# Load stage with split constants and two issuing queues, and the first expert's gathers moved into the routing block

## The reference, cut to what matters

```python
    logits = jnp.einsum('bsh,eh->bse', x, router_w) + router_b
    topk_vals, topk_idx = jax.lax.top_k(softmax(logits), 2)
    ...
    sorted_indices = jnp.argsort(-expert_mask, axis=0)[:cap]        # cap = 512
    used_idx = (sorted_indices * sorted_mask).reshape(-1)
    inputs = x_flat[used_idx] * sorted_mask                          # rows gathered by index
    h = relu(einsum('ceh,ehi->cei', inputs, experts_inter))          # 7 experts, 128 -> 512
    out = einsum('cei,eih->ceh', h, experts_out) * in_w              # 512 -> 128
    combined = zeros.at[used_idx].add(out)                           # rows scattered by index
    combined = combined + x_flat * (noop_w * noop_mask)
    ...
    x = x + layernorm(attention(layernorm(x), Wq, bq, Wk, bk, Wv, bv, Wo, bo))   # the first layer
```

## Time and profile before

| | us |
|---|---|
| median of three runs | 1279.82 |
| lowest and highest of them | 1271.53, 1280.86 |
| the profiled execution, its own time | 1281.18 |
| its span in the trace | 1279.4 |
| the load block, to the first instruction of the next | 15.16 |
| `route`, to the first instruction of `capped_mixture` | 1124.01 to 1157.29 |
| `capped_mixture`, to the end | 1157.29 to 1279.4 |

### The profile page before, as it was taken

The page is one execution under the profiler, slowest core; times in us unless marked ns, Lnnn a source line. Parts: engine busy times, 40 slices in busy tenths (PEclk is TensorE's granted clock), DMA queues, the critical chain, the costliest instruction groups (busy, mean ns, idle before and its releaser), DMA issues. The chain is left out here.

```text
span 1279.4 us, 33612 instructions
## 1 busy us (share of the span) xinstructions
PE 1126.1 (88%) x11807; PEld 633.0 (49%) x11807; DVE 997.9 (78%) x2742; ACT 849.6 (66%) x1826; POOL 657.2 (51%) x680
## 2 busy tenths in 40 slices
PE   3879999999999997999999999789999999617766
PEld 2334444444444443566666666445666665414552
DVE  2679999999999983888898889459999998782213
ACT  1468888888888885555555565268999998522204
POOL 3213444454433310556655666547888887505653
PEclk9889999999999998999999999899999999858987
DMA  4231111111111110000000000013122111041117
GB/s 113 62 93 32 32 28 30 32 31 28 34 32 31 34 30 1 2 2 2 2 1 2 1 2 1 4 37 96 49 56 55 37 40 31 18 133 34 44 40 197
DMA packets 83141, 48.91 MB, mean 38 GB/s; under 512 B 17111, under 2 KB 80032, under 8 KB 82976
## 3 DMA queue, kind: packets, MB, share of 16 engines
q1 hardware_dynamic: 80496, 42.62, 12.5%
q0 software_dynamic: 1792, 3.70, 1.1%
q10 hardware_dynamic: 688, 0.44, 0.1%
HBM read 16.51 MB, written 10.26 MB: 21 GB/s over the span
## 5 line engine op out<-in xcount | busy, mean ns | idle before, releaser
L577 DVE TENSOR_REDUCE mxsS<-scoreS 128x2 f32<-128x512 f32 x512 | 329.0, 685 | 44.0 <-PE scoreS L685 38.8
L473 ACT ACTIVATE PTS<-stS 128x512 f32<-128x512 f32 x512 | 283.4, 591 | 58.4 <-PE stS L689 58.2
L1833 POOL TENSOR_TENSOR ghid<-gprod,ghid 128x512 f16<-128x512 f32 x144 | 165.4, 1159 | 122.3 <-ACT ghid L1946 120.7
L685 PE MATMUL scoreS<-QK 31*128 31x256 f16 x1024 | 170.9, 282 | 27.6 <-DVE mxsS L577 12.0
L885 POOL TENSOR_TENSOR PTP<-PTP,EP 128x512 f32<-128x512 f32 x128 | 162.8, 1283 | 53.0 <-ACT PTP L1061 52.8
L689 PE MATMUL stS<-QK 32*128 32x256 f16 x1024 | 167.2, 279 | 1.3 <-ACT PTS L473 1.3
L705 PE MATMUL pvS<-PTS,Vx 128*32 128x256 f32 x2048 | 141.1, 394 | 0.6 <-ACT PTS L473 0.4
L1946 ACT ACTIVATE ghid<-gprod 128x512 f16<-128x512 f32 x144 | 90.1, 626 | 69.8 <-DVE gprod L2041 69.7
L1215 DVE TENSOR_SCALAR AP<-score_psP 128x768 int32<-128x768 int32 x128 | 121.6, 950 | 17.3 <-PE score_psP L1354 16.5
L685 PEld LDWEIGHTS scoreS<-QK 31*128 31x128 f16 x1024 | 53.1, 93 | 148.1 <-DVE mxsS L577 90.2
L1061 ACT ACTIVATE PTP<-AP,epsP 128x768 f32<-128x768 f32 x128 | 119.2, 931 | 3.0 <-DVE AP L1215 2.4
(11 more groups left out here) (322 smaller groups left out, 2244.0 us busy)
## 6 DMA issues: line engine op xcount, KB each, us to landing
QK<-HLS SPq DMA_DIRECT2D x384, 32.0 KB, 1.9
QK<-HLP SPq DMA_DIRECT2D x192, 32.0 KB, 1.9
expert_outputs<-tzero SPq DMA_DIRECT2D x8, 512.0 KB
cgot<-expert_outputs SPq DMA_DIRECT2D x16, 256.0 KB, 5.2
tokens<-XB SPq DMA_DIRECT2D x16, 128.0 KB, 2.8
out_dram<-X SPq DMA_DIRECT2D x8, 256.0 KB, 2.3
wi<-L_ffn_experts_inter_dram SPq DMA_DIRECT2D x1, 1792.0 KB, 8.4
wo<-n_L_ffn_experts_out_dram SPq DMA_DIRECT2D x7, 256.0 KB, 3.3
```

Source lines behind the costliest of these rows:

```text
L473: act.activation(PT[:, n % NPT, :], st_ps[:, (NS * t + n) % 3, :], ACT.Exp, scale=SCALE).then_inc(s_exp, 1)
L577: dve.tensor_reduce(mxs[:, u // 4, :, at], score_ps[:, n % 2, :].rearrange("p (c s) -> p c s", c=TC), AX.X, ALU.max).then_inc(s_max, 1)
L685: scored = pe.matmul(score_ps[:, k, cols], QK[part, new, g, 0, rows], QK[part, new, g, 1, :], start=True, stop=True)
L1833: pool.tensor_tensor(hid[:, n // FC % NHID, 1, c, :], prod[:, n % NPROD, :], hid[:, n // FC % NHID, 0, c, :], ALU.subtract).then_inc(s_hid, 1)
```

## The change

In the load block the constants come as two DMAs, the identity first. A new semaphore `s_first` counts that piece and the four weights of the first layer; PE waits for these five (80) and turns four weights. DVE then waits for the rest (`s_rows` at 64: three weights, second piece of constants, two gates) ahead of `spread_v`; PE's matmuls with `wo` and the biases and DVE's copies of `bo` and `bias1` come next, and the other three weights and the gates are turned and copied last. The seven late loads leave SP's list and stand at the end of ACT's, behind the copies of `ones`.

In `route`, POOL waits for `s_clear` (9 DMAs) and for DVE's index casts and issues the four gathers of expert 0 there, on a semaphore `s_xe0` that is allocated outside both blocks. `capped_mixture` begins with gather 1. PE gets 16 matmuls without a reader at the end of `route` and keeps 4 of its 24 in `capped_mixture`.

```diff
@@ load_weights
         def _(sp):
             for k, src in enumerate([dram["L0_attn_Wq"], dram["L0_attn_Wk"], dram["L0_attn_Wv"], dram["L0_attn_Wo"]]):
-                sp.dma_start(rows[:, k, :], src).then_inc(s_rows, 16)
+                sp.dma_start(rows[:, k, :], src).then_inc(s_first, 16)
...
-            for k, name in enumerate(["L0_ffn_wq", "L0_ffn_wk", "L0_ffn_wv"]):
-                sp.dma_start(arriving.flat[:, k, :], dram[name]).then_inc(arriving.s_flat, 16)
-            sp.dma_start(weights[1]["wo"][:], dram["L0_ffn_wo"]).then_inc(arriving.s_flat, 16)
-            sp.dma_start(arriving.route0[:], dram["L0_ffn_router_w"]).then_inc(arriving.s_flat, 16)
-            sp.dma_start(w["norm2"][:], dram["L0_ffn_norm2_w"].rearrange("(d a) -> d a", a=1)).then_inc(arriving.s_flat, 16)
-            sp.dma_start(arriving.norm[:, 0:1], dram["L0_ffn_norm1_w"].rearrange("(d a) -> d a", a=1))\
-                .then_inc(arriving.s_flat, 16)
 
         @block.scalar
         def _(act):
-            act.dma_start(cst[:], dram["constants"]).then_inc(s_rows, 16)
+            act.dma_start(cst[:, 0:C_TRI], dram["constants"][:, 0:C_TRI]).then_inc(s_first, 16)
+            act.dma_start(cst[:, C_TRI:C_ALL], dram["constants"][:, C_TRI:C_ALL]).then_inc(s_rows, 16)
...
             for k in range(3):
                 act.dma_start(QK[SHIFT_LAST:P:32, k, :, 1, :], ones[:]).then_inc(s_one, 16)
+            for k, name in enumerate(["L0_ffn_wq", "L0_ffn_wk", "L0_ffn_wv"]):
+                act.dma_start(arriving.flat[:, k, :], dram[name]).then_inc(arriving.s_flat, 16)
...
             act.wait_ge(s_one, 48)
...
         def _(pe):
-            pe.wait_ge(s_rows, 128)
-            for k in range(len(names)):
+            pe.wait_ge(s_first, 80)
+            for k in range(4):
                 pe.transpose(turned[:, k, 0:P], rows[:, k, :], cst[:, 0:P]).then_inc(s_turned, 1)
-            pe.transpose(turned[:, 7, 0:H + NE], gates[:], cst[0:H + NE, 0:H + NE]).then_inc(s_turned, 1)
-
             pe.wait_ge(s_spread, 1)
...
+            pe.wait_ge(s_rows, 64)
+            for k in range(4, len(names)):
+                pe.transpose(turned[:, k, 0:P], rows[:, k, :], cst[:, 0:P]).then_inc(s_turned, 1)
+            pe.transpose(turned[:, 7, 0:H + NE], gates[:], cst[0:H + NE, 0:H + NE]).then_inc(s_turned, 1)
...
             dve.wait_ge(s_bias, 80)
+            dve.wait_ge(s_rows, 64)
             dve.tensor_scalar(spread_v[:], cst[:, C_TRI + P:C_TRI + 2 * P], bias_v[:, 0:1], None, ALU.mult)\
                .then_inc(s_spread, 1)
+            dve.wait_ge(s_out, 1)
+            dve.tensor_copy(weights[0]["bo"][:], turned[:, 0, 0:D])
+            dve.wait_ge(s_out, 2)
+            dve.tensor_copy(w["bias1"][:], turned[:, 1, 0:NE])
             for k, name in ((4, "wq"), (5, "wk")):
...
-            dve.wait_ge(s_out, 1)
-            dve.tensor_copy(weights[0]["bo"][:], turned[:, 0, 0:D])
-            dve.wait_ge(s_out, 2)
-            dve.tensor_copy(w["bias1"][:], turned[:, 1, 0:NE])
@@ route
             pool.wait_ge(s_zero, 5)
+            pool.wait_ge(s_clear, 16 * (2 * NT * D // (P * 1024) + 1))
+            pool.wait_ge(s_v, marks["index"])
+            for t in range(CAP // P):
+                pool.indirect_dma_start(xe[:, 0, t, :], None, yd, bass.IndirectOffsetOnAxis(ap=idx_in[:, t:t + 1], axis=0),
+                                        bounds_check=NT - 1, oob_is_err=False).then_inc(s_xe0, 16)
...
             last.then_inc(s_p, 1)
+            for _ in range(16):
+                pe.matmul(ps[:, 2, :], cstb[:, 0:P], cstb[:, P:2 * P].unsqueeze(1).to_broadcast([P, 4, P]),
+                          start=True, stop=True)
@@ capped_mixture
-            gather(0)
             gather(1)
             gather(2)
...
-            for _ in range(24):
+            for _ in range(4):
                 pe.matmul(hid_ps[:, 0, :], cstb[:, 0:P], cstb[:, P:2 * P].unsqueeze(1).to_broadcast([P, 4, P]),
                           start=True, stop=True)
             turn(0)
```

More of the change, by code:

```diff
@@ L1450, in load_weights @@
         turned = ctx.enter_context(nc.psum_tensor("turned", [P, 8, 512], F32))
+        s_first = sem("s_first")
         s_rows = sem("s_rows")
@@ L1489, in _ @@
                 act.dma_start(QK[SHIFT_LAST:P:32, k, :, 1, :], ones[:]).then_inc(s_one, 16)
+            for k, name in enumerate(["L0_ffn_wq", "L0_ffn_wk", "L0_ffn_wv"]):
+                act.dma_start(arriving.flat[:, k, :], dram[name]).then_inc(arriving.s_flat, 16)
+            act.dma_start(weights[1]["wo"][:], dram["L0_ffn_wo"]).then_inc(arriving.s_flat, 16)
+            act.dma_start(arriving.route0[:], dram["L0_ffn_router_w"]).then_inc(arriving.s_flat, 16)
+            act.dma_start(w["norm2"][:], dram["L0_ffn_norm2_w"].rearrange("(d a) -> d a", a=1)).then_inc(arriving.s_flat, 16)
+            act.dma_start(arriving.norm[:, 0:1], dram["L0_ffn_norm1_w"].rearrange("(d a) -> d a", a=1))\
+                .then_inc(arriving.s_flat, 16)
             act.wait_ge(s_one, 48)
@@ L1533, in _, with route @@
             dve.tensor_copy(w["router1"][:], turned[:, 7, H:H + NE])
-            dve.wait_ge(s_out, 1)
-            dve.tensor_copy(weights[0]["bo"][:], turned[:, 0, 0:D])
-            dve.wait_ge(s_out, 2)
-            dve.tensor_copy(w["bias1"][:], turned[:, 1, 0:NE])
-def route(nc, cst, chosen, idx_in, idx_out, pick, noop, xe, yd, od):
+def route(nc, cst, cstb, chosen, idx_in, idx_out, pick, noop, xe, s_xe0, yd, od):
     T, LATE, BY_ACT = NTILE, slice(NTILE - 2 * TC, NTILE), 14
@@ L1667, in _ @@
             lk(dve.tensor_copy(idx_out[:], to[:, 0, :]), dve.tensor_copy(idx_in[:], to[:, 1, :]))
+            marks["index"] = lk.k
         @block.gpsimd
@@ L2098, in _, with capped_mixture @@
             dve.wait_ge(s_res, NBLK)
-def capped_mixture(nc, idx_in, idx_out, pick, noop, xe, Y, X, cst, cstb, wi, wo, out, yd, od):
+def capped_mixture(nc, idx_in, idx_out, pick, noop, xe, s_xe0, Y, X, cst, cstb, wi, wo, out, yd, od):
     NX, TB, FC = NE - 1, CAP // P, F1 // P
@@ L2107, in capped_mixture @@
     with ExitStack() as ctx:
-        take = semaphores(nc, ctx)
+        take = semaphores(nc, ctx, held=[s_xe0])
         def sb(name, shape, dt=F32):
@@ L2130, in capped_mixture @@
         s_ready = sem("s_ready")
-        s_xe = [sem(f"s_xe{k}") for k in range(3)]
+        s_xe = [s_xe0] + [sem(f"s_xe{k}") for k in (1, 2)]
         s_turn = sem("s_turn")
@@ L2397, in build @@
         noop = sb("noop", [P, NTILE], F32)
-        route(nc, cst, chosen, idx_in, idx_out, pick, noop, xe, yd, od)
-        capped_mixture(nc, idx_in, idx_out, pick, noop, xe, XB, X, cst, cstb, wi, wo, out, yd, od)
+        s_xe0 = nc.alloc_semaphore("s_xe0")
+        route(nc, cst, cstb, chosen, idx_in, idx_out, pick, noop, xe, s_xe0, yd, od)
+        capped_mixture(nc, idx_in, idx_out, pick, noop, xe, s_xe0, XB, X, cst, cstb, wi, wo, out, yd, od)
 def kernel(**inputs):
```

## The result

The changed kernel takes 1281.57 us (median of 20 runs, 1275.54 to 1291.41) against 1278.43 for the kernel before (20 runs, 1271.53 to 1283.16), a ratio of 1.0033 with the interval 1.0017 to 1.0049 (the medians alone give 1.0025). The forecast was 1277.9: a small gain, and it came out as a small loss, inside the range that was recorded (1269.3 to 1282.0) and on the other side of no change. The profiled execution had 1281.76, 1.9 over its span of 1279.9. Ratios leave out executions over 1.5% above the fastest of their kernel, and one profile here, that of `e9`, is of such an execution.

The account below looks back on a forecast made before the run. It took SP's issuing to bound the load block and POOL's gathers to bound the mixture. Load -2.45 plus seam +0.5 gave -1.95 us, from 1279.82 to 1277.9 us, range 1269.3 to 1282.0.

Parts of the forecast that it names:

- The sum's sign: Whole kernel: load block -2.45 us plus seam +0.5 us gives -1.95 us, a small gain.
- The crossing adds 0.92: Seam before the mixture: POOL's last gather ends at 1162.40, the crossing adds 0.92, so the mixture begins at 1163.3.
- +1.5 as the upper bound: Seam: most it could cost, if the clock falls while PE idles; the value taken was +0.5 us.
- The load block's 2.45: Load block: ends with DVE at 11.81 instead of SP at 14.26, 2.45 us less; next block starts at about 12.7.
- rival 1: Load block: the seven issues stall on ACT as long as on SP, no gain there; 1280.3 us, chance 0.13.
- I take 2.45, since before DVE found the biases there without a wait: Load block: biases taken as landed in time, so spread_v starts at 8.03 and the block gains 2.45 us.
- The bound written beside it: Load block: biases land by 9.8, spread_v starts 1.8 later, block ends at 13.6, 0.7 us less than before.
- Rival 2, the clock: Seam: the clock falls while PE idles and rises only after up 0, costing about 3.4 us; 1281.3 us, chance 0.10.
- The idle stretch: Seam: PE idle between the 16 matmuls in route and the four in the mixture, forecast at 1.5 to 3.5 us.
- Rival 3, the unnamed wait of the mixture: Mixture: the 16.21 us unnamed wait may hold 8 us that go, or faster runs dominate; about 1269.6 us, chance 0.20.
- Does the middle keep its length?: Unedited middle of the kernel: assumed to keep its length when it starts 2.4 us earlier, else the prediction is wrong.
- The base.: Starting time of the forecast: the kernel before at 1279.82 us, the median of three runs.

Follow-up runs that it names:

- e9: Load edits alone on the kernel before, biases first on ACT, then the ones constants with their own semaphore, spread_v waiting only for these; ratio 1.0041 [1.0012, 1.0070].
- e5: Routing and mixture edits alone on the kernel before, plus a 0.97 us memset on POOL behind the four gathers; ratio 1.0036 [1.0014, 1.0059].
- e10: Routing and mixture edits alone on the kernel before, with only the first of expert 0's four gathers in route; ratio 1.0037 [1.0016, 1.0058].
- e11: Routing and mixture edits alone on the kernel before, with eight gathers (two experts) in route; ratio 1.0047 [1.0017, 1.0076].
- e7: Routing and mixture edits alone on the kernel before, with 32 dummy matmuls in route instead of 16; ratio 1.0020 [0.9994, 1.0047].
- e6: Load edits alone on the kernel before, with the five biases issued directly behind the first piece of constants; ratio 1.0036 [1.0005, 1.0067].
- e8: Load block edits alone on the kernel before, run a second time; ratio 1.0016 [0.9987, 1.0046].
- e2: The changed kernel, unedited, once more, against the kernel before; ratio 1.0012 [0.9986, 1.0038].
- e4: Only the edits of route and capped_mixture on the kernel before, old load block; ratio 0.9997 [0.9972, 1.0022].
- e12: The changed kernel, unedited, once more on chip C, against the kernel before; ratio 1.0017 [0.9996, 1.0038].
- e16: Only the edits of route and capped_mixture on the kernel before, a second time, on chip D; ratio 1.0034 [1.0008, 1.0059].
- e3: Only the edits of load_weights on the kernel before, routing and mixture as before; ratio 1.0001 [0.9980, 1.0021].
- e15: Load block edits alone on the kernel before, a third time, on chip D; ratio 1.0006 [0.9976, 1.0036].

## Why the prediction was wrong

- **The sum's sign.** Forecast: -2.45 + 0.5 = -1.95. By the stages: -1.2 for the load block and +1.2 to +2.9 for the seam, so 0 to +1.7 us or a ratio of 1.000 to 1.0013. Measured for the changed kernel: 1.0033, 1.0012 and 1.0017 (the lower ends of their intervals 1.0017, 0.9986, 0.9996). The direction is explained; the rest of the first one, 0.0004 or more even from its lower end, is not. Before against itself gave 0.9972 and 0.9985, so a comparison can be off by that much.
- **The step that failed first: "The crossing adds 0.92", counted from the end of POOL's last gather.** This is the term of the seam that was mis-sized: gather 1 came 2.07 later instead of 0.5. The crossing is 0.8 to 1.1, but it begins when the gathers have landed, 2.5 to 2.9 after the last one starts. Before, POOL had no gather under way when it left `route`, so no row of that trace priced this wait. But the earlier trace rows have the landing (2.62), and the fourth gather started 4.20 behind the first, so a bound was there to be had: 1156.37 + 0.79 to the first gather + 4.20 + 2.62 + 0.92 for the crossing + 0.89 = 1165.8, against 1163.67. That is +2.1, which is what came. I put +1.5 as the upper bound, and for another cause. `e5`, `e10` and `e11` show the wait, and the DRAIN shows its end. The rest of this mechanism held: the delay of gather 1 is carried through the mixture. The first scatter of expert 3 starts at 58.8 behind the cast in the changed kernel and at 58.9 in `e7`, against 56.7 in `e6` and `e8`.
- **The load block's 2.45.** SP's issuing did end the block, ACT issues without a stall (0.45 to 0.47 each, so rival 1 is out), and DVE is what is late next. The step that failed is "I take 2.45, since before DVE found the biases there without a wait". The last bias had landed at 8.69 before, behind the 8.03 that I took for `spread_v`; that no wait was seen at 9.34 says only that DVE was busy until then. In the changed order it lands at 9.79. The bound written beside it, biases late and the block ending at 13.6, is what happened (13.57). The value between was -0.8 to -1.8 in the six profiles. A second term was left out: I let ACT be done with its issues at 9.95, but its list ends with the wait for the copies of `ones`, and it comes to the barrier at 12.24. SP came there at 14.44, so even with early biases no more than 2.2 was to be had, and `e9` shows ACT as the last one.
- **Rival 2, the clock.** Its mechanism happened: the clock fell to 0.50 in or right behind an idle stretch of PE of 4.1 to 10.1 us in all profiles of the new seam but that of `e7`, where that stretch was 1.33, and `up` 0 took 5.7 to 6.5 in `e2`, `e4`, `e5`, `e10`, `e11`, `e12` and `e16`. In the changed kernel's own profile it was at 0.50 from 1171.7 to 1175.1 and back up for `up` 0. The idle stretch was forecast at 1.5 to 3.5 us and was 5.32, by the same missed wait of POOL. Its price was too high: 3.4 on all that follows, against the 1.1 to 1.4 above. That its time of 1281.3 lies beside the measured 1281.57 is luck.
- **Rival 3, the unnamed wait of the mixture.** There is such time, about 6 us, and the profile after is without it. But kernels of both kinds have it on chips A and D and neither has it on B and C, so nothing here makes it an effect of the change. It also fits the medians of before: 1284.9 and 1283.9 on A and D, 1276.7 and 1277.6 on B and C. Why some chips show it stays open.
- **"Does the middle keep its length?"** It varies from 1139.8 to 1152.2 though nothing in it was edited (1159.8 in `e9`, whose clock was at 0.50 for 48 us from 842 on, left out of the means here). With the load edits its mean is some 3 to 4 us longer, with a scatter as large. Whether the load edits themselves lengthen the middle is left open. It would explain the rest of the first ratio, and that all five ratios of load edits with the old seam lie above 1 (1.0001, 1.0036, 1.0016, 1.0041, 1.0006) though their next block starts earlier.
- **The base.** The forecast was tied to a median of three runs, 1279.82; with 20 runs before has 1278.43.

No version here beats the kernel before. By its stages the best is the load edits with the old seam (`e3`, `e8`, `e15`), 1.2 us or 0.1% shorter at the start, which three comparisons of 12 runs each cannot tell from zero and none of them shows as a gain.

## What to carry to other kernels

Before moving an indirect DMA ahead of a block's end, add its landing to the barrier: here POOL, which issued it, came to the barrier when its DRAIN had ended, 0.21 us behind the landing, and to the next block 2.42 behind its last gather; the other engines waited with it (PE was idle for 5.32). The early issue was worth nothing here, since POOL's first task in the next block is more issues: gather 1 came at 9.37 instead of 7.30.

When an edit removes the engine that was last, look for the latest transfer that each of the others waits for, and take its landing (the last update of its semaphore) and not the absence of a wait as the value. When a delay seems to be absorbed, follow it stage by stage: here 1.3 us were there at `turn` 6, until a fall of the clock elsewhere hid them. For effects under 0.3%, run the kernel before against itself first, and compare profiles stage by stage on one chip.

## What the runs showed of the hardware

- POOL's DRAIN at the end of a block ends 0.09, 0.21 or 0.37 us behind the landing of its last gather with one, four or eight gathers ahead (waits of 2.36, 2.42 and 2.60 us), and its first instruction of the next block follows 0.69 later; 0.97 us of other work on POOL fits into that wait.
- Biases issued at 2.8 to 4.6 us landed late beside the bulk: `spread_v` found them at 8.9 to 9.8 in every profile with the change's order. Issued first, they had landed at 5.4 (`e6`), and at 6.92 `spread_v` started when all that it needs went first, and then `gates` landed at 11.1.
- Two queues did not stall together in the changed kernel: while SP's last two chunks of x took 4.45 us to issue (from 4.82), ACT's issues from 6.78 on took 0.45 to 0.47 each.
- Behind 4.5 us of idling the granted clock was 0.50 in the first 4.6 us of `up` 0 (`e12`), which took 5.96 instead of 3.70, and 1.1 to 1.4 of that were left late in the mixture.
- On two of four chips the mixture is about 6 us longer in each profile, with a DVE wait of 13.3 to 16.2 us that ends 4.2 to 5.3 behind the end given for the matmul that it waits for; on the other two it never is.
